# Second LayerNorm and gate in groups of 2, 5 and 7 tiles, with denominators per group, GpSimd products per tile and expert weights loaded between the groups

## The reference

```python
x = x + gnn(_layernorm(x), ...)          # attention over the edges of each node
x = x + ffn(_layernorm(x)[None], ...)[0] # gate, two experts of eight

def gnn(x, ...):
    ...
    alpha = ea / (denom[dst] + 1e-16)
    msg = (v[src] + e) * alpha[:, :, None]
    out = jax.ops.segment_sum(msg, dst, num_segments=n)
    return out.reshape(n, H * C) + (x @ Ws + bs)

def ffn(x, ...):
    gate_logits = x_flat @ Wg + bg + bias
    topk_vals, topk_idx = jax.lax.top_k(gate_logits, TOP_K)
    topk_w = jax.nn.softmax(topk_vals, axis=-1)
    ...
    h = jax.nn.relu(jnp.einsum('td,edh->teh', x_flat, W1) + b1)
    y = jnp.einsum('teh,ehd->ted', h, W2) + b2
    ...
```

## Time and profile before

| | us |
|---|---|
| median of 3 runs | 2683.87 |
| lowest and highest of them | 2682.81, 2685.87 |
| profiled execution, its own time | 2682.07 |
| its span | 2680.3 |
| busy: PE, PEld, DVE, ACT, POOL | 2422.3, 1966.7, 2024.4, 1571.2, 1795.5 |
| the stage of the change (2026.4 to 2123.8 in the trace) | 97.4 |

### The profile page before, as it was taken

One profiled execution on the slowest core, in us unless ns is written; L12 is line 12 of the kernel. 1 busy time (PEld: TensorE's weight loads), 2 busy tenths in 40 slices (PEclk: granted clock), 3 DMA queues, 4 the chain that ended last, 5 costly groups with the idle time before them and its releaser, 6 DMA issues. The chain is left out here.

```text
span 2680.3 us, 69447 instructions
## 1 busy us (share of the span) xinstructions
PE 2422.3 (90%) x14102; PEld 1966.7 (73%) x14103; DVE 2024.4 (76%) x5180; ACT 1571.2 (59%) x4380; POOL 1795.5 (67%) x2179
## 2 busy tenths in 40 slices
PE   5996899999999999999999999999994659999980
PEld 2443688888788888888888888878863549999970
DVE  5765799999999999999999999989987671111116
ACT  1222477767677777767777677767762226666650
POOL 4232588888888888888888888888874025555540
PEclk9998999999999999999999999999995579999995
DMA  6323777777777777777777777777743602222218
GB/s 214 110 96 119 212 225 225 221 225 226 219 227 225 223 222 227 223 226 226 227 224 224 226 222 228 225 212 226 227 140 100 218 24 67 70 70 70 71 57 288
DMA packets 327794, 489.52 MB, mean 183 GB/s; under 512 B 54506, under 2 KB 249180, under 8 KB 327148
## 3 DMA queue, kind: packets, MB, share of 16 engines
q0 software_dynamic: 81152, 259.63, 33.8%
q1 hardware_dynamic: 239244, 213.23, 25.4%
q10 hardware_dynamic: 7056, 12.85, 1.5%
HBM read 437.21 MB, written 49.61 MB: 182 GB/s over the span
## 5 line engine op out<-in xcount | busy, mean ns | idle before, releaser
L761 POOL DMA_INDIRECT kv_ring<-vk_table,tab_c x880 | 875.4, 995 | 283.5 <-issue 215.3
L916 PE MATMUL ps_e<-we_sb,aT 128*128 128x256 f32 x3520 | 915.3, 383 | 14.1 <-DVE ve_ke L1007 11.2
L1001 DVE TENSOR_TENSOR ve_ke<-kv_ring,ps_e 128x512 f32<-128x512 f32 x880 | 601.2, 683 | 80.8 <-issue 33.5
L916 PEld LDWEIGHTS ps_e<-we_sb,aT 128*128 128x128 f32 x3520 | 602.6, 191 | 67.8 <-issue 14.6
L771 POOL TENSOR_TENSOR w_ring<-ve_ke,ea 128x264 f32<-128x264 f32 x880 | 567.2, 648 | 22.2 <-PE ps_u L968 6.2
L968 PE MATMUL ps_u<-w_ring,sel 128*128 128x264 f32 x1760 | 541.6, 389 | 10.3 <-DVE acc L1067 4.6
L849 ACT COPY aT<-ps_t 128x256 f32<-128x256 f32 x880 | 326.3, 371 | 348.0 <-PE ps_t L904 220.4
L920 PE MATMUL ps_e<-q_parts,selT 128*128 x2640 | 433.3, 273 | 0.0
L1067 DVE TENSOR_TENSOR acc<-acc,ps_u 128x264 f32 x880 | 369.3, 420 | 25.5 <-issue 10.1
L988 DVE TENSOR_REDUCE alpha<-ve_ke 128x8 f32<-128x256 f32 x880 | 365.7, 416 | 6.4 <-issue 3.9
L1007 DVE TENSOR_TENSOR ve_ke<-ve_ke,ps_e 128x256 f32<-128x256 f32 x880 | 361.1, 410 | 1.9
(11 more groups left out here) (249 smaller groups left out, 2646.8 us busy)
## 6 DMA issues: line engine op xcount, KB each, us to landing
a_ring<-in_edge_attr SPq DMA_DIRECT2D x880, 128.0 KB
loc_c<-loc_table SPq DMA_DIRECT2D x220, 128.0 KB
kv_ring<-vk_table,tab_c POOLq DMA_INDIRECT x880
vk_table<-kv_out SPq DMA_DIRECT2D x49, 256.0 KB
q_parts<-y_table ACTq DMA_DIRECT2D x49, 256.0 KB, 3.8
skip_table<-skip_out SPq DMA_DIRECT2D x49, 128.0 KB
q_parts<-skip_table SPq DMA_DIRECT2D x7, 896.0 KB, 7.1
xn_table<-acc SPq DMA_DIRECT2D x7, 896.0 KB, 4.9
```

The costliest lines, as they stand in the source:

```text
L761: g.indirect_dma_start(out=kv_ring[:, i % N_KV, :], out_offset=None, in_=vk_table, in_offset=bass.IndirectOffsetOnAxis(ap=tab_c[:, c % N_T ...
L916: t.matmul(ps_e[i % 2][:, 0:D], aT[i % 2][:, k * P:(k + 1) * P], we_sb[:, k, :], start=(k == 0), stop=(k == KD - 1))
L1001: v.tensor_tensor(both, kv.rearrange("p (t h c) -> p t h c", t=2, c=C), by_head(e, C)[:, None, :, :].to_broadcast([P, 2, H, C]), ALU.add). ...
```

## The change

The change is made in the block of suffix 4 alone:

- the groups are of 2, 5, and then six times 7 tiles, eight in all;
- the denominators and their reciprocals are made per group (`denominators(g)`): three groups ahead of measure(0), and each later group's ahead of a measure, two groups before its use;
- POOL multiplies tile by tile, 49 instructions, and waits once per group for its reciprocals;
- DVE goes measure(g), normalise(g) without the measure of the next group in between, and the bias rows are added at the end;
- root(g+1) stands in ACT's program behind the copy of the fourth tile of group g (or of its last, where it has fewer);
- each load of expert weights is issued behind the store of a group: W1 behind groups 0 and 1, W2 behind groups 2 to 5;
- `measure` and `normalise` work on as many columns as the group has tiles.

```diff
-            groups = [(j, min(SG, NT - j)) for j in range(0, NT, SG)]
+            groups = [(0, 2), (2, SG - 2)] + [(j, min(SG, NT - j)) for j in range(SG, NT, SG)]
...
                     sp.wait_ge(xn_ready, j + n)
                     sp.dma_start(xn_table[j * P:(j + n) * P, :].rearrange("(j p) d -> p j d", p=P),
                                  xn2[:, j:j + n, 0:D]).then_inc(xn_stored, 16)
-
-                for k in range(KD):
-                    sp.dma_start(w1_sb[:, k, :].rearrange("p (e f) -> p e f", e=NE),
...
+                    if g < KD:
+                        sp.dma_start(w1_sb[:, g, :].rearrange("p (e f) -> p e f", e=NE),
...
+                    elif g < KD + KF:
+                        sp.dma_start(w2_sb[:, g - KD, :].rearrange("p (e f) -> p e f", e=NE),
...
-                pool.wait_ge(den_step, 2)
-                for j, n in groups:
-                    a, b = j * H, (j + n) * H
-                    nc.gpsimd.tensor_tensor(x1_heads[:, a:b, :], heads[:, a:b, 0:C], inv[:, a:b][:, :, None].to_broadcast([P, b - a, C]),
-                                            ALU.mult).then_inc(att_ready, 1)
+                for g, (j, n) in enumerate(groups):
+                    pool.wait_ge(den_ready, g + 1)
+                    for t in range(j, j + n):
+                        a, b = t * H, (t + 1) * H
+                        nc.gpsimd.tensor_tensor(x1_heads[:, a:b, :], heads[:, a:b, 0:C], inv[:, a:b][:, :, None].to_broadcast([P, H, C]),
+                                                ALU.mult).then_inc(att_ready, 1)
...
                 for g, (j, n) in enumerate(groups):
-                    if g + 1 < NGR:
-                        root(g + 1)
                     for t in range(j, j + n):
...
                         nc.scalar.copy(xnT[t % 2][:, :], ps_t[t % 2][:, 0:D]).then_inc(xnT_ready, 1)
+                        if t == j + min(n - 1, 3) and g + 1 < NGR:
+                            root(g + 1)
...
-                dve.wait_ge(loaded, 16 * 3)
-                v.tensor_tensor(bias_sb[:, :], bg_sb[:, :], gb_sb[:, :], ALU.add).then_inc(bias_ready, 1)
-                measure(0)
-                for g in range(NGR):
-                    if g + 1 < NGR:
-                        measure(g + 1)
-                    normalise(g)
+                def denominators(g):
+                    a, b = groups[g][0] * H, sum(groups[g]) * H
+                    then(v.tensor_scalar(den[:, a:b], heads[:, a:b, C:CP].rearrange("p n c -> p (n c)"), 1e-16, None, ALU.add))
+                    v.reciprocal(inv[:, a:b], den[:, a:b]).then_inc(den_ready, 1)
+
+                for g in range(3):
+                    denominators(g)
+                measure(0)
+                normalise(0)
+                for g in range(1, NGR):
+                    if g + 2 < NGR:
+                        denominators(g + 2)
+                    measure(g)
+                    normalise(g)
+                dve.wait_ge(loaded, 16 * 3)
+                v.tensor_tensor(bias_sb[:, :], bg_sb[:, :], gb_sb[:, :], ALU.add).then_inc(bias_ready, 1)
```

More of the change, by code:

```diff
@@ L1130, in gnn_ffn @@
             loaded = sem("loaded4", c4)
-            den_step = sem("den_step", c4)
+            den_ready = sem("den_ready", c4)
             bias_ready = sem("bias_ready", c4)
@@ L1169, in _ @@
                                  xn2[:, j:j + n, 0:D]).then_inc(xn_stored, 16)
-                for k in range(KD):
-                    sp.dma_start(w1_sb[:, k, :].rearrange("p (e f) -> p e f", e=NE),
[L1173 to L1176, removed]
+                    if g < KD:
+                        sp.dma_start(w1_sb[:, g, :].rearrange("p (e f) -> p e f", e=NE),
+                                     W1[:, g * P:(g + 1) * P, :].rearrange("e p f -> p e f")).then_inc(experts_loaded, 16)
+                    elif g < KD + KF:
+                        sp.dma_start(w2_sb[:, g - KD, :].rearrange("p (e f) -> p e f", e=NE),
+                                     W2[:, (g - KD) * P:(g - KD + 1) * P, :].rearrange("e p f -> p e f")).then_inc(experts_loaded, 16)
+                assert NGR >= KD + KF
                 sp.wait_ge(xn_stored, 16 * NGR)
@@ L1190, in root @@
                     act.wait_ge(var_ready, g + 1)
-                    nc.scalar.activation(sd[:, g % 2, :], vp[:, g % 2, :], ACT.Sqrt).then_inc(sd_ready, 1)
+                    nc.scalar.activation(sd[:, g % 2, 0:groups[g][1]], vp[:, g % 2, 0:groups[g][1]], ACT.Sqrt).then_inc(sd_ready, 1)
                 root(0)
                 for g, (j, n) in enumerate(groups):
-                    if g + 1 < NGR:
-                        root(g + 1)
                     for t in range(j, j + n):
@@ L1240, in measure @@
                     par = g % 2
-                    dve.wait_ge(att_ready, g + 1)
+                    dve.wait_ge(att_ready, j + n)
                     dve.wait_ge(skip_loaded[par], 16 * (g // 2 + 1))
@@ L1256, in normalise @@
                     dve.wait_ge(sd_ready, g + 1)
[L1257 to L1261, removed]
+                    then(v.reciprocal(r0[:, 0:n], sd[:, par, 0:n]))
+                    then(v.tensor_tensor(r1[:, 0:n], r0[:, 0:n], r0[:, 0:n], ALU.mult))
+                    then(v.tensor_tensor(r2[:, 0:n], r1[:, 0:n], vp[:, par, 0:n], ALU.mult))
+                    then(v.tensor_scalar(r3[:, 0:n], r2[:, 0:n], -0.5, 1.5, ALU.mult, ALU.add))
+                    then(v.tensor_tensor(rstd[:, 0:n], r0[:, 0:n], r3[:, 0:n], ALU.mult))
                     for t in range(n):
```

2 lines of the change are left out of this document (1 added, 1 removed).

## The result

The changed kernel takes 2666.83 us in the median of four runs (2663.56 to 2670.03), against 2683.41 before (2682.81 to 2685.87): a ratio of 0.9936, with a 95% interval from 0.9919 to 0.9954. On another chip five more runs gave 2659.96 against 2672.81, a ratio of 0.9949 (0.9935 to 0.9963). So the change gains 0.5 to 0.6 of a per cent, little but clear of the noise. The forecast was 2672.5, the range 2665.5 to 2680. The profiled execution took 2670.03 us and has a span of 2668.2.

What follows compares the result with a forecast made beforehand. The stage was taken as four parts with different limits (PE idle, PE and DVE busy, PE catching up, only DMA), SP ending it. 5.4 us from PE's end plus 6.0 from SP's gave 11.4: 2672.5 us, range 2665.5 to 2680.

Steps and rivals of the forecast that it cites:

- start: Stage's beginning: both tiles of group 0 normalised by 2036.3, so PE starts 20.5 us earlier than now.
- DVE's pace: Groups 2 to 7: DVE's period of 8.83 us or more sets the pace; PE keeps 5.4 us of its gain.
- SP's tail: Stage's end: with weight loads behind stores, 0.57 + 0.5 us follow L1279 instead of 7.07, 6.0 us less.
- period with denominators: DVE's time per group of seven, groups 2 to 5, including denominators, reciprocal and waits for POOL: 10.13 us.
- POOL's tile: POOL's product for one tile of 256 columns: about 0.60 us, bounds 0.46 and 0.64.
- The wait for POOL in groups 2 to 5: L1251 and one or two small DVE instructions wait for POOL: 0.6 us per group, bounds 0 and 1.2.
- the denominators' pair: On DVE, one group's denominators and their reciprocal: 0.24 + 0.46 = 0.70 us per group, groups 1 to 5.
- The exposed square root: Without look-ahead DVE sees the root's whole way, 0.45 us instead of 0.08: period 8.46 becomes 8.83.
- ACT and PE at the end: From the last epsilon's end to L1279, with eight transpose and gate pairs left: 11.8 us.
- the cover: Skip load 3, the tightest: issued about 2038.5, landed by 2047, used at 2055.6; 8 us to spare.
- starvation: Rival: POOL gets ahead, DVE waits for all seven tiles, 4.2 us instead of 0.6; 2693.5 us, chance 0.07.
- The smaller waits: Rival: DVE's waits for POOL are smaller, 3.5 to 4 us less; 2668.5 us (2664 to 2669), chance 0.20.

Runs made afterwards that it cites:

- The first experiment: Kernel before, with only SP's six weight loads moved behind the stores of groups 0 to 5: 2683.2 against 2676.7 us, ratio 1.0025, stage 102.53 us.
- the second experiment: Kernel before, with weight loads behind the stores plus the changed order of DVE and ACT: 2682.05 against 2685.66 us, ratio 0.9986, stage 92.11 us.

## Why the prediction was right, and where its steps were off

The way and the three terms (start, DVE's pace, SP's tail) were right, and the gain in the stage was forecast 3.0 us too small. The first median lies 5.7 us under the forecast, near the lower end of the range; the stage accounts for 3.0 of that and the rest lies outside it. On the second chip the medians differ by 12.9 us, 1.5 more than forecast.

| step, us from the stage's start | forecast | measured |
|---|---|---|
| PE's first transpose | 10.0 | 8.8 |
| addition of group 1 | 10.5 | 9.8 |
| addition of group 2 | 19.0 | 18.1 |
| period with denominators | 10.13 | 9.56 |
| period without | 8.83 | 8.83 |
| last epsilon's end | 72.9 | 69.8 |
| from there to the gate sums' reading | 11.8 | 12.2 |
| from there to the next stage | 1.07 | 0.87 |

- **POOL's tile** was put at 0.60 us; it takes 0.615, and one is started every 0.57. The 0.04 between a duration and the spacing was taken off the 0.637 of 264 columns, so 0.60 was a spacing, and it is 0.03 too large.
- **The wait for POOL in groups 2 to 5** is the term that was mis-sized: 0.6 us was forecast, and 0.08 is left of the period's 9.56 after 8.83 and the 0.65 of the denominators' pair (0.70 was put). Half of POOL's overhang of 1.2 us behind the statistics was laid on DVE's small instructions. In the rows above the overhang is 0.9 us (2060.40 to 2061.28), and the way of the square root over ACT, 0.45 us which the same sum had just made visible, lies in it, and so do L1252 and the reciprocal. Four groups make 2.3 us (2.1 of them the waits, 0.2 the pairs) and the start up to the addition of group 2 another 0.9. The end takes 0.2 back, and with that it is the 3.0.
- **The exposed square root** was right to 0.01: the period of group 6 is 8.83.
- **ACT and PE at the end**: 12.2 for 11.8. From the epsilon's end to the gate 0.82 us pass instead of 0.6, since the first copy starts 0.35 us behind the start of the square root and not beside it, and from there to the next transpose 0.87 instead of 0.7.
- **SP's tail**: 6.2 instead of 6.0. In the prediction it stands as a gain of the moved loads alone. The first experiment shows that it is one only together with the order without look-ahead; moved alone, the loads cost 11.4 and win 6.2. The prediction did work out the cover (8 us for load 3) for the changed order, and there it held: issued at 2039.02, landed 9.2 us later, used at 2055.41, with 7.2 us to spare. It did not say that the order was what gave it.
- **The rivals**: DVE did get its turn after each POOL instruction in all kernels, with grains of 0.6 us and of 3.2, so starvation is out. The smaller waits came true in their size, 3.0 us for the 3.5 to 4 of that rival, but by neither of its conditions: instructions of L1263's form do wait for POOL (1.29 us for two in group 0, 3.80 for seven with all denominators first), and POOL's tile takes 0.57 and not 0.46. From group 1 on the changed kernel's find POOL idle. The median of 2666.83 falls in that rival's span of 2664 to 2669; by the stage alone it would be 2669.4, just inside the forecast's own 2669 to 2677.
- What the prediction said of PE, that it gains 20 us at its start and keeps 5, was right in kind: it gains 21.7 and keeps 8.2, and groups of seven, with a later start, keep more.

The stage by steps, each kernel with one part more: 97.3 before, 102.5 with the weight loads moved, 92.1 with the order, 81.6 with the denominators per group and their place, the bias rows and the tiles' products, 82.9 with the first group split. The step from 92.1 to 81.6 is 10.6 us, and the two profiles tell where: 4.4 us at the first addition, which no longer stands behind the small loads and the bias rows (9.65 us into the stage, now 5.20), and 8.4 between the first two additions, where POOL's 3.2 us instructions had held DVE's small ones (20.25 us, now 11.87). Of these 12.8 us the denominators' pairs and the small waits take 2.3 back later. How the 8.4 are shared between the rationing and the products' grain was not run.

## What to carry to other kernels

A queue that is last at a barrier is worth emptying, but count for each load that is moved ahead of another how long after its issue the other is used: an order of the consumers that looks slower, without look-ahead, can be what pays for the move. Where another engine works behind the groups, look also at what it still has before it when the last group is measured: one group here without look-ahead, two with it. An early start of an engine that is not the limit is not kept. Where two engines hinder each other, ration the one that is ahead, and put its share beside instructions that it does not hinder; the size of its instructions then mattered little here (0.4 us).

## What the runs showed of the hardware

DVE and POOL took turns exactly: in the rows of the second experiment, L1251, L1258, L1259 and L1260, of 0.17 us each beside an idle POOL, took 2.65 to 3.19 us. None waited for more than one POOL instruction of 3.2 us, although POOL's next was ready. The reciprocal between them (L1257) took 0.20 us and waited for none. Statistics with one input (L1247, 2.39 us for seven) took the same beside a busy POOL as beside an idle one (2.38 in the earlier trace rows). The normalising instructions, with two scalars by pointer, did wait: 3.80 us for seven, with POOL busy beside most of them, against 2.35. The Trainium skill (SBUF — State Buffer, Who interferes with whom) says that a DVE instruction with at most one SBUF input, outside the two-port modes, does not contend with GpSimd, and that in a two-port mode one engine holds the shared ports for its whole instruction and the other blocks fully. The statistics, the reciprocal and the waits of a whole POOL instruction agree with this; in which mode an instruction ran, no row shows. The rows add that a waiting DVE instruction comes before POOL's next.

PE's clock was granted at 0.50, the level of 1.2 GHz, in the whole stage in all twelve profiles, after 15 us or more without work and also where PE was busy 99% of 8.6 us. A skip load of 896 KB took 7.1 us to land with the weights at the end of the queue (median of seven), 8.5 in the changed kernel (median of six), and 12.5 in the first experiment behind a load of 2 MB.
